# The first transposes of a graph-network stack taken from TensorE to blocked loads and VectorE

## The chip, the cores and the metric

The kernel runs on one core of one Trainium2 chip. The metric is device time in microseconds of one execution. The kernel before takes 1293.59 us, the median of three runs (1293.4 to 1294.62).

## The reference, cut to what matters

Four graph layers run over 64 independent graphs of 128 nodes with 256 features. Each is followed by a residual sum and a layer norm. Only the first touches what is changed here, apart from the adjacency, which all use:

```python
x:   (64, 128, 256) float32      adj: (64, 128, 128) float32, entries 0 or 1
qkv = x @ W_qkv                              # 8 heads of 64
attn = softmax(q @ k.T * scale) * 0.33 + 0.33 * adj + 0.33 * exp(-adj)     # masked
x = layernorm(x + (attn @ v) @ W_out + b_out)
# layer 1: H = (adj != 0), two hypergraph convolutions; layer 2: attention weights adj * exp(leaky(...)),
# two products with them; layer 3: adj @ (x @ W)
```

## The kernel before

The work goes in 32 groups of G = 2 graphs, and the engines follow orders written out by hand. One turn of the main loop (`group(i, j, n)` in each engine's block) holds the front half of group i (attention and first norm, F), the back half of group j = i - 1 (layers 1 to 3, B), and the lead of group n = i + 1 (L: x transposed and the first two of four query and key products). A function `first()` in each block takes the set-up, the weights, the front of group 0 and the lead of group 1. The turns with a lead after that are 30 (n from 2 to 31); then come one turn without a lead and one with a back half alone.

A product in float32 is made of three TensorE products of a float32r high part and low part of each operand: high times high, high times low, low times high (L405, L406, L409; for queries and keys L494, L495, L498). So whatever TensorE multiplies is copied once to a high part, by ScalarE, and once subtracted to a low part, mostly by VectorE.

TensorE contracts over partitions, so x and adj are needed transposed. Before, per group:

- `xT0_(n)` on TensorE (L483): four 128x128 transposes of `xin` into bank 0 of PSUM. ScalarE copies them to `xT0` high (L846), VectorE subtracts to `xT0` low (L1198, a helper's line, which the low parts of others share). `qk_(n, 0)`, `qk_(n, 1)` and, a turn later, `qk_(i, 2)`, `qk_(i, 3)` and `v_` read both.
- `adjT_(n)` on TensorE (L476): two transposes of `adj_in` into bank 6, after a wait for `dve_o3`. ScalarE copies them to `adjT` (L842), VectorE makes `HT` of it at the start of the next turn (`incidence`, L1222).

The orders in a turn around these, as far as the prediction's steps touch them:

- TensorE: ..., `xT2_(j)` (L604), `PT_(i, 0)` (L538), `xT0_(n)` (L483), `Z_(j, 0)`, `Z_(j, 1)` (L405, L406, L409), `si_(j, 0)`, `si_(j, 1)` (L632), `PV_(i, 0)` (L548), `qk_(n, 0)`, ..., `T3_(j, 0)`, `AT_(i)` (L513), `adjT_(n)` (L476), `T3_(j, 1)` (L661, L663, L665), ...
- VectorE: ..., `norm_(0, 1)` (four operations on L1285), `bn1_(0)` (L1347), `mv1_(0)` (L1208), `bn1_(1)`, `xT2_` (low part, L1198), `rl_`, `mv1_(1)`, `norm_(1, 0)`, `Z_(0)` (L1364, gives `sji`), `norm_(1, 1)`, `z0_(0)` (L1370), `Z_(1)` (L1364), `z2_(0)`, `xT0_` of n (low part), `z2_(1)`, ...; at the end `o3_(0)` (L1447), `zb_(1)` (L1203), ...
- GpSimd: `resid_` of the front (L1739), `resid_(0)`, `aT_`, `resid_(1)`, `gate_`, `rsh_`, then `rs1_(0)` and `rs1_(1)` (each L1722, L1726, L1732), `rs2_`, ...
- SyncE loads `xin` and the mask at the start of a turn, `adj_in` and `wrow` when their readers have finished, near its end (`reload`).

`si_(j, 1)` waits for `dve_sj` of `Z_(1)`; the low products in `Z_(j, 0)` wait for `dve_xT2`.

Of the kernel before, what the change touches and what calls it, by code (L numbers as in the profile page):

```python
# [5 lines left out]
F32 = mybir.dt.float32  # L6
# [3 lines left out]
ALU = mybir.AluOpType  # L10
# [16 lines left out]
def gnn_stack_kernel(nc, x, adj, nodemask, W_qkv, W_out, b_out, W1, b1, gamma, beta, W2, b2,  # L27
# [13 lines left out]
    QKB = 2 * INNER // P  # L41
    SCALE = float(DH) ** -0.5
# [3 lines left out]
    with ctx:  # L46
# [105 lines left out]
        adjT = at("adjT", [P, G, P])  # L152
        xT0 = pair("xT0", [P, DC, G, P])
# [33 lines left out]
        bank_adjT = 6  # L187
        bank_xT0 = 0
# [22 lines left out]
        def sem(name):  # L211
# [134 lines left out]

        block = ctx.enter_context(nc.Block())

        @block.sync
        def _(sp):  # L350
            sp.dma_start(wqkv_raw[:].rearrange("p c h t d -> p c (h t d)"),
                         W_qkv.rearrange("(c p) n -> p c n", p=P)).then_inc(ld_wqkv, 16)
            sp.dma_start(xin[:], xg[:, 0:G, :]).then_inc(x_in, 16)
            sp.dma_start(w2_raw[:], W2.rearrange("(c p) n -> p c n", p=P)).then_inc(ld_w2, 16)
            sp.dma_start(adj_in[:], ag[:, 0:G, :]).then_inc(a_in, 16)
            sp.dma_start(w1_raw[:], W1.rearrange("(c p) n -> p c n", p=P)).then_inc(ld_w1, 16)
# [11 lines left out]
            def reload(i):  # L368

                sp.wait_ge(pe_xT0, i)  # L370
                sp.wait_ge(pool_resid0, i)
                sp.sem_inc(sp_past, 1)
                sp.dma_start(xin[:], xg[:, bass.ds(i * G, G), :]).then_inc(x_in, 16)
                sp.wait_ge(act_mbc, i * G)
# [5 lines left out]
                sp.wait_ge(pe_adjT, i)  # L380
# [21 lines left out]
        def _(pe):  # L402
# [70 lines left out]
            def adjT_(i):  # L473
                pe.wait_ge(a_in, i * 16 + 16)
                for g in range(G):
                    last = pe.transpose(PS[:, bank_adjT, g * P:(g + 1) * P], adj_in[:, g, :], ident[:])  # L476
                last.then_inc(pe_adjT, 1)

            def xT0_(i):
                pe.wait_ge(x_in, i * 16 + 16)  # L480
                for c in range(DC):
                    for g in range(G):
                        last = pe.transpose(PS[:, bank_xT0, (c * G + g) * P:(c * G + g + 1) * P],  # L483
                                            xin[:, g, c * P:(c + 1) * P], ident[:])
                last.then_inc(pe_xT0, 1)

            def qk_(i, k):
                pe.wait_ge(act_xT0, i + 1)
                for m in range(2 * k, 2 * k + 2):
# [6 lines left out]
                    pe.wait_ge(dve_xT0, i + 1)  # L496
# [4 lines left out]
            def v_(i, g):  # L501
# [3 lines left out]
                pe.wait_ge(dve_xT0, i + 1)  # L505
# [161 lines left out]
            def group(i, j, n):  # L667
# [35 lines left out]
                if L:  # L703
                    after(pe, act_v, 2, s, 2)
                    xT0_(n)
# [13 lines left out]
                if L:  # L719
                    qk_(n, 1)  # L720
# [26 lines left out]
                if L:  # L747
                    after(pe, dve_o3, 2, s - 1, 1)
                    adjT_(n)
# [7 lines left out]
            def first():  # L757

                pe.wait_ge(ident_ok, 2)
                xT0_(0)  # L760
                w2_transposes()
                mask_column()
                pe.wait_ge(set_hi, QK_DONE)
# [54 lines left out]
        def _(act):  # L818
# [170 lines left out]
            def group(i, j, n):  # L989
# [74 lines left out]
                if L:  # L1064
                    adjT_(n)
# [796 lines left out]
```

## Time and profile before

| | |
|---|---|
| median of three runs | 1293.59 us (1293.4 to 1294.62) |
| span of the profiled execution | 1291.5 us |
| own time of the profiled execution | not listed apart from the three runs |
| TensorE busy | 1247.2 us, 97% |
| VectorE busy | 1068.8 us, 83% |
| ScalarE busy | 971.6 us, 75% |
| GpSimd busy | 478.5 us, 37% |
| mean granted TensorE clock | 0.993 |

A turn of the main loop takes 38.5 us; the one looked at is that from 640.0 to 678.5 us, in which the four engines are busy 38.27, 32.73, 29.97 and 14.66 us. The timeline gives for each instruction (or run of like ones, x4) its start, its length, engine, line, and what is written from what. Instructions of one engine overlap a little: what counts for the next is the distance from start to start. An idle stretch ahead of an instruction stands behind it in brackets, with what ended it.

### The profile page before, as it was taken

Reading aid. Unit: us, or ns where it says so; the run is one execution under the profiler, and the core shown is the slowest. Engines: PE = TensorE matmul, PEld = TensorE weight load, DVE = VectorE, ACT = ScalarE, POOL = GpSimd, SP = SyncE. Lnnn points to the kernel's source line nnn. Section 1 sums busy time; section 2 is a strip of 40 time slices with the busy share of each in tenths; the row PEclk is TensorE's granted clock in tenths of the full one; section 3 lists DMA queues with packets and bytes.
Section 4 is the critical chain, followed back from the end, with each engine's and each line's share of the span. In section 5 each row is a group of like instructions: output and inputs, shape, how many; then the busy total and the mean of one; then the engine's idle time right before and its main releaser. Section 6 shows DMA issues by size and latency. Waiting matters only on the chain.

```text
span 1291.5 us, 32910 instructions
## 1 busy us (share of the span) xinstructions
PE 1247.2 (97%) x9589; PEld 1110.3 (86%) x9589; DVE 1068.8 (83%) x3399; ACT 971.6 (75%) x2806; POOL 478.5 (37%) x1126
## 2 busy tenths in 40 slices
PE   6799999999999999999999999999999999999985
PEld 5688888888888888888898888898888898888874
DVE  3688888888888898888898888888888888888885
ACT  5477877777877777877777787778787777787773
POOL 3233444333443333443333343333343433344432
PEclk9899999999999999999999999999999999999998
DMA  6000100000000000000000100000001000000000
GB/s 214 17 8 21 26 25 25 16 16 18 25 25 25 22 11 17 25 25 25 25 9 17 25 25 25 25 8 19 23 25 25 25 8 23 20 25 25 17 9 9
DMA packets 44293, 32.52 MB, mean 25 GB/s; under 512 B 8176, under 2 KB 43120, under 8 KB 44272
## 3 DMA queue, kind: packets, MB, share of 16 engines
q1 hardware_dynamic: 42688, 31.47, 8.4%
q0 software_dynamic: 176, 0.52, 0.2%
q10 hardware_dynamic: 1408, 0.27, 0.1%
q8 instruction: 10, 0.16, 0.1%
q14 instruction: 11, 0.09, 0.0%
HBM read 23.87 MB, written 8.39 MB: 25 GB/s over the span
## 4 chain that ended last, share of the span: by engine, by line
PE 93%; DVE 3%; ACT 1%; issue 1%; DMA 1%; POOL 0%; DVEq 0%; SPq 0%; POOLq 0%; ACTq 0%
PE PS L405 15%; PE PS L406 15%; PE PS L409 15%; PE PS L494 5%; PE PS L548 5%; PE PS L495 5%; PE PS L498 5%; PE PS L528 4%; PE PS L538 4%; PE PS L584 3%; PE PS L568 2%; PE PS L598 2%; PE PS L520 2%; DVE ysb L1447 1%; PE PS L611 1%; PE PS L604 1%
## 5 line engine op out<-in xcount | busy, mean ns | idle before, releaser
L1722 POOL TENSOR_TENSOR rs<-mv,eps_c 128x1 f32<-128x1 f32 x256 | 61.2, 239 | 582.9 <-DVE mv L1208 581.4
L1726 POOL TENSOR_TENSOR rs<-rs,mhalf 128x1 f32<-128x1 f32 x320 | 176.3, 551 | 25.3
L891 ACT ACTIVATE prob<-PS,neg_max 128x128 f32<-128x128 f32 x512 | 179.7, 416 | 2.0 <-DVE neg_max L1272 2.0
L1285 DVE SCALAR_TENSOR_TENSOR prob<-prob,rl,gate 128x128 f32<-128x128 f32 x512 | 145.6, 347 | 1.5
L494 PE MATMUL PS<-xT_hi,wqk_hi 128*128 128x256 f32 x512 | 141.3, 297 | 0.0
L495 PE MATMUL PS<-xT_hi,wqk_lo 128*128 128x256 f32 x512 | 134.9, 285 | 0.0
L891 ACT ACTIVATION_READ_ACCUMULATOR prob<-PS,neg_max 128x1 f32 x512 | 131.4, 257 | 0.0
L1319 DVE SCALAR_TENSOR_TENSOR hid<-PS,Dn,b_bc 128x512 f32<-128x512 f32 x64 | 48.1, 751 | 85.4 <-PE PS L409 85.4
L498 PE MATMUL PS<-xT_lo,wqk_hi 128*128 128x256 f32 x512 | 103.5, 284 | 0.0
L494 PEld LDWEIGHTS PS<-xT_hi,wqk_hi 128*128 128x128 f32 x512 | 98.2, 192 | 5.3 <-issue 5.0
L495 PEld LDWEIGHTS PS<-xT_hi,wqk_lo 128*128 128x128 f32 x512 | 98.7, 193 | 0.0
L898 ACT ACTIVATE probT<-PS 128x1024 f32<-128x1024 f32 x64 | 65.9, 1029 | 32.0 <-PE PS L538 32.0
L909 ACT ACTIVATE x<-ysb,rs 128x256 f32<-128x256 f32 x128 | 73.5, 602 | 19.8 <-POOL rs L1732 19.8
L1732 POOL TENSOR_SCALAR rs<-mv,rs 128x1 f32<-128x1 f32 x256 | 68.2, 266 | 53.0 <-POOL rs L1726 52.6
L405 PE MATMUL PS<-wk_hi,xT_hi 128*128 128x260 f32 (+1 forms) x256 | 83.6, 348 | 0.7 <-ACT xT_hi L950 0.7
L406 PE MATMUL PS<-wk_lo,xT_hi 128*128 128x260 f32 (+1 forms) x256 | 83.4, 337 | 0.0
L498 PEld LDWEIGHTS PS<-xT_lo,wqk_hi 128*128 128x128 f32 x512 | 80.3, 192 | 0.0
L1272 DVE TENSOR_REDUCE neg_max<-PS 128x8 f32<-128x1024 f32 x64 | 77.9, 1219 | 1.9 <-PE PS L528 1.9
L1208 DVE BATCH_NORM_AGGREGATE mv<-st 128x2 f32<-128x6 f32 x320 | 56.5, 176 | 25.1 <-DVE st L1324 9.9
L874 ACT ACTIVATE qk<-PS 128x512 f32<-128x512 f32 x128 | 72.6, 591 | 5.3 <-PE PS L498 5.3
L909 ACT ACTIVATE xout<-ysb,rs 128x256 f32<-128x256 f32 x64 | 38.5, 601 | 47.2 <-POOL rs L1732 47.2
L1198 DVE TENSOR_TENSOR xT_lo<-PS,xT_hi 128x256 fp32r<-128x256 f32 (+1 forms) x128 | 70.5, 551 | 3.9 <-ACT xT_hi L846 1.8
(225 smaller groups left out, 4227.3 us busy)
## 6 DMA issues: line engine op xcount, KB each, us to landing
xin<-in_x_dram SPq DMA_DIRECT2D x32, 256.0 KB, 2.7
out_dram<-xout SPq DMA_DIRECT2D x32, 256.0 KB, 2.2
adj_in<-in_adj_dram SPq DMA_DIRECT2D x32, 128.0 KB, 2.1
wrow<-in_adj_dram SPq DMA_DIRECT2D x32, 128.0 KB, 4.5
wqkv_raw<-in_L_gnn_W_qkv_dram SPq DMA_DIRECT2D x1, 1536.0 KB, 7.6
w_raw<-in_L_gnn_W_dram SPq DMA_DIRECT2D x3, 512.0 KB, 11.4
mask_bc<-in_nodemask_dram SPq DMA_DIRECT2D x32, 32.0 KB, 2.8
wk_raw<-in_L_gnn_Wk_dram SPq DMA_DIRECT2D x3, 256.0 KB, 9.0
```

What stands on the lines that cost most here:

```text
L405: pe.matmul(dst, lhs[0], rhs[0], start=start, stop=False)
L406: pe.matmul(dst, lhs[0], rhs[1], start=False, stop=False)
L409: return pe.matmul(dst, lhs[1], rhs[0], start=False, stop=stop)
L494: pe.matmul(dst, w[0], xT0[0][:, c], start=(c == 0), stop=False)
L495: pe.matmul(dst, w[1], xT0[0][:, c], start=False, stop=False)
L498: last = pe.matmul(dst, wqk[0][:, c, t, h:h + 2], xT0[1][:, c], start=False, stop=(c == DC - 1))
L874: act.activation(qk[:, 2 * k:2 * k + 2].rearrange("p m g n -> p (m g n)"), PS[:, bank_qk[k], :], copy, scale=SCALE if k < 2 else 1.0).then ...
L891: last = act.activation(prob[:, t, h, :], PS[:, bank, k * P:(k + 1) * P], ACT.Exp, bias=neg_max[:, t, h:h + 1], accum_out=row_sum[:, t, h: ...
L909: act.activation(dst, src, ACT.Identity, scale=rs[:, n, g, 1:2], bias=rs[:, n, g, 0:1]).then_inc(done, 1)
L1272: dve.tensor_reduce(neg_max[:, t], scores, AX_X, ALU.max, negate=True).then_inc(dve_max, 1)
L1285: last = dve.scalar_tensor_tensor(prob[:, t, h, :], prob[:, t, h, :], rl[:, t, h:h + 1], gate[:, t], ALU.mult, ALU.add)
L1726: return pool.tensor_tensor(rs[:, n, g, 1:2], rs[:, n, g, 0:1], mhalf[:], ALU.pow)
```

## The change

x and adj are each loaded a second time, in blocks of 32x32: the block of rows 32a.. and columns 32k.. goes to partitions 32k.., to the place in the row that belongs to a. One VectorE `transpose`, which transposes inside each 32x32 block, then gives the whole transposed matrix in SBUF. The blocks come in runs of 32 floats (128 bytes), 2048 of them for x and 1024 for adj in a group, in four loads each. The low part of x goes from VectorE to GpSimd. The transposes on TensorE, their two PSUM uses, and ScalarE's copy of adj leave; ScalarE's copy to `xT0` high now reads SBUF.

```diff
+        Q = 32; QB = P // Q
+        def x_block(i, k):
+            return x[bass.ds(i * G, G)].rearrange("g (a r) (c k w) -> k r c (g a) w", r=Q, k=QB, w=Q)[k]
+        def adj_block(i, k):
+            return adj[bass.ds(i * G, G)].rearrange("g (a r) (k w) -> k r (g a) w", r=Q, k=QB)[k]
...
             # SyncE, set-up: after wqkv_raw, ahead of xin; and after adj_in
+            for k in range(QB):
+                sp.dma_start(xblk[k * Q:(k + 1) * Q], x_block(0, k)).then_inc(xb_in, 16)
...
             def reload(i):
-                sp.wait_ge(pe_xT0, i)
                 sp.wait_ge(pool_resid0, i)
                 sp.sem_inc(sp_past, 1)
                 sp.dma_start(xin[:], xg[:, bass.ds(i * G, G), :]).then_inc(x_in, 16)
+                sp.wait_ge(dve_xT, i)
+                for k in range(QB):
+                    sp.dma_start(xblk[k * Q:(k + 1) * Q], x_block(i, k)).then_inc(xb_in, 16)
+                sp.wait_ge(dve_adjT, i)
+                for k in range(QB):
+                    sp.dma_start(ablk[k * Q:(k + 1) * Q], adj_block(i, k)).then_inc(ab_in, 16)
                 sp.wait_ge(act_mbc, i * G)
...
             # TensorE
-                    pe.wait_ge(dve_xT0, i + 1)          # in qk_ and v_
+                    pe.wait_ge(pool_xT0, i + 1)
...
                 if F:
                     PT_(i, 0)
-                if L:
-                    after(pe, act_v, 2, s, 2)
-                    xT0_(n)
...
                 if L:
+                    after(pe, act_v, 2, s, 2)
                     qk_(n, 1)
...
                     AT_(i)
-                if L:
-                    after(pe, dve_o3, 2, s - 1, 1)
-                    adjT_(n)
...
             # ScalarE
             def xT0_(i):
-                act.wait_ge(pe_xT0, i + 1)
-                act.activation(xT0[0][:].rearrange("p c g n -> p (c g n)"), PS[:, bank_xT0, :], copy).then_inc(act_xT0, 1)
+                act.wait_ge(dve_xT, i + 1)
+                act.wait_ge(pe_v, i * G)
+                act.wait_ge(pool_xT0, i)
+                act.activation(xT0[0][:]..., xT[:]..., copy).then_inc(act_xT0, 1)
...
             # VectorE
+                def xT_():
+                    dve.wait_ge(xb_in, (i * QB + QB) * 16)
+                    dve.wait_ge(act_xT0, i)
+                    dve.wait_ge(pool_xT0, i)
+                    dve.transpose(xT[:]..., xblk[:]...).then_inc(dve_xT, 1)
                 def incidence():
-                    dve.wait_ge(act_adjT, i + 1)
+                    dve.wait_ge(ab_in, (i * QB + QB) * 16)
+                    dve.wait_ge(act_adjTb, i)
+                    dve.transpose(adjT[:]..., ablk[:]...).then_inc(dve_adjT, 1)
+                    dve.wait_ge(dve_adjT, i + 1)
+                    dve.wait_ge(act_BHT, i * G)
+                    dve.wait_ge(pe_AT, i)
                     dve.tensor_scalar(HT[:], adjT[:], 0.0, None, ALU.not_equal).then_inc(dve_HT, 1)
...
                     norm_(0, 1)
+                if L:
+                    front(n)[1]()                      # xT_
                 if B:
                     bn1_(0)
...
                     z2_(0)
-                if L:
-                    front(n)[1]()                      # the low part of x
                 if B:
                     z2_(1)
...
             # GpSimd
+                def xlow_():
+                    pool.wait_ge(act_xT0, i + 1)
+                    pool.wait_ge(pe_v, i * G)
+                    pool.tensor_tensor(xT0[1][:]..., xT[:]..., xT0[0][:]..., ALU.subtract).then_inc(pool_xT0, 1)
...
                     rs1_(1)
+                if L:
+                    front(n)[2]()                      # xlow_
+                if B:
                     rs2_(0)
```

In `first()` the same calls move: VectorE's `front(1)[1]()` keeps its place behind `centre_w3` and now is the transpose; ScalarE's `xT0_(1)` keeps its place ahead of `OT_(0, 0)`; GpSimd's low part for group 0 comes first and that for group 1 behind `gate_products`.

## Rows read from the trace of the kernel before

**Rows 1.** The page: TensorE's busy time, and the chain that ended last

```profile
PE 1247.2 (97%) x9589; PEld 1110.3 (86%) x9589; DVE 1068.8 (83%) x3399; ACT 971.6 (75%) x2806; POOL 478.5 (37%) x1126
...
PE 93%; DVE 3%; ACT 1%; issue 1%; DMA 1%; POOL 0%; DVEq 0%; SPq 0%; POOLq 0%; ACTq 0%
```

**Rows 2.** Timeline, TensorE, the middle of a turn: start us, length us, instruction

```profile
655.02 0.60 PE L483 MATMUL PS<-ident,xin 128*128 128x128 f32 x4
655.38 0.36 PE L405 MATMUL PS<-wk_hi,xT_hi 128*128 128x260 f32 x1
...
656.86 0.85 PE L409 MATMUL PS<-wk_hi,xT_lo 128*128 128x260 f32 x4
...
659.65 0.38 PE L632 MATMUL PS<-ident,sji 128*128 128x128 f32 x2
659.96 1.09 PE L548 MATMUL PS<-probT,vh 128*64 128x128 f32 x16
```

**Rows 3.** Timeline, ScalarE, the same stretch

```profile
654.41 0.65 ACT L950 ACTIVATE xT_hi<-PS 128x512 fp32r<-128x512 f32 x1
```

**Rows 4.** Timeline around `adjT_`, all engines

```profile
674.67 0.48 DVE L1203 SCALAR_TENSOR_TENSOR zb_lo<-PS,rs,zb_hi 128x256 fp32r<-128x256 f32 x1
674.79 0.20 PEld L476 LDWEIGHTS PS<-ident,adj_in 128*128 128x128 f32 x2 [0.42 <-DVE ysb L1447]
...
675.31 0.29 PE L665 MATMUL PS<-zb_lo,aT_hi 128*128 128x256 f32 x1
```

**Rows 5.** Timeline, VectorE, the middle of the turn

```profile
654.01 0.42 DVE L1347 BATCH_NORM_STATS2 st<-ysb 128x6 f32<-128x256 f32 x1
...
655.10 0.69 DVE L1198 TENSOR_TENSOR xT_lo<-PS,xT_hi 128x512 fp32r<-128x512 f32 x1
...
656.03 1.14 DVE L1285 SCALAR_TENSOR_TENSOR prob<-prob,rl,gate 128x128 f32<-128x128 f32 x4
...
657.44 1.13 DVE L1285 SCALAR_TENSOR_TENSOR prob<-prob,rl,gate 128x128 f32<-128x128 f32 x4
...
659.39 0.22 DVE L1364 SCALAR_TENSOR_TENSOR sji<-PS,rs,gate_c 128x4 f32<-128x4 f32 x1 [0.42 <-PE PS L409]
...
659.92 0.68 DVE L1198 TENSOR_TENSOR xT_lo<-PS,xT_hi 128x512 fp32r<-128x512 f32 x1
```

**Rows 6.** Groups of instructions by line and form, VectorE: busy us, mean ns, idle before

```profile
L1319 DVE SCALAR_TENSOR_TENSOR hid<-PS,Dn,b_bc 128x512 f32<-128x512 f32 x64 | 48.1, 751 | 85.4 <-PE PS L409 85.4
...
L1138 DVE TENSOR_REDUCE w3m<-w_raw 128x4 f32<-128x1024 f32 x1 | 1.2, 1214 | 0.0
...
L1131 DVE COPY beta_bc<-beta_c 128x512 f32<-128x512 f32 x1 | 0.4, 418 | 0.0
```

**Rows 7.** Timeline, GpSimd, the middle of the turn

```profile
654.85 0.19 POOL L1722 TENSOR_TENSOR rs<-mv,eps_c 128x1 f32<-128x1 f32 x1 [5.43 <-DVE mv L1208]
...
656.10 0.34 POOL L1722 TENSOR_TENSOR rs<-mv,eps_c 128x1 f32<-128x1 f32 x1
...
657.27 0.27 POOL L1732 TENSOR_SCALAR rs<-mv,rs 128x1 f32<-128x1 f32 x1 [0.21 <-POOL rs L1726]
```

**Rows 8.** Timeline, set-up: long GpSimd subtractions

```profile
44.84 3.77 POOL L1716 TENSOR_TENSOR wk_lo<-wk_raw,wk_hi 128x512 fp32r<-128x512 f32 x3 [14.96 <-DVE wk_raw L1155]
```

**Rows 9.** Timeline, VectorE, the same stretch

```profile
46.52 0.88 DVE L1173 TENSOR_TENSOR gate_c<-bsum,ab_bc 128x1 f32<-128x1 f32 x1
```

**Rows 10.** One line of the kernel: durations in ns, minimum, median, maximum

```profile
L1432 DVE TENSOR_SCALAR degb<-degf x32: 158/159/367, 60.3 to 1254.8; 128x2 f32<-128x2 f32 x32
```

**Rows 11.** DMA queues, and issues with us to landing

```profile
q1 hardware_dynamic: 42688, 31.47, 8.4%
...
xin<-in_x_dram SPq DMA_DIRECT2D x32, 256.0 KB, 2.7
...
mask_bc<-in_nodemask_dram SPq DMA_DIRECT2D x32, 32.0 KB, 2.8
```

**Rows 12.** The chain that ended last, set-up: start us, us, what

```profile
1.75 11.39 DMA w_raw<-in_L_gnn_W_dram
```

More of the change, by code:

```diff
@@ L41, in gnn_stack_kernel @@
     QKB = 2 * INNER // P
+    Q = 32
+    QB = P // Q
     SCALE = float(DH) ** -0.5
@@ L152, in gnn_stack_kernel @@
         adjT = at("adjT", [P, G, P])
+        ablk = at("ablk", [P, G * QB, Q])
+        xblk = at("xblk", [P, DC, G * QB, Q])
+        xT = at("xT", [P, DC, G * QB, Q])
         xT0 = pair("xT0", [P, DC, G, P])
@@ L373, in reload @@
                 sp.dma_start(xin[:], xg[:, bass.ds(i * G, G), :]).then_inc(x_in, 16)
+                sp.wait_ge(dve_xT, i)
+                sp.sem_inc(sp_past, 1)
+                for k in range(QB):
+                    sp.dma_start(xblk[k * Q:(k + 1) * Q], x_block(i, k)).then_inc(xb_in, 16)
+                sp.wait_ge(dve_adjT, i)
+                sp.sem_inc(sp_past, 1)
+                for k in range(QB):
+                    sp.dma_start(ablk[k * Q:(k + 1) * Q], adj_block(i, k)).then_inc(ab_in, 16)
                 sp.wait_ge(act_mbc, i * G)
@@ L471, in gate_sums @@
                 last.then_inc(set_pe, 1)
[L473 to L485, printed above, removed]
             def qk_(i, k):
@@ L759, in first @@
                 pe.wait_ge(ident_ok, 2)
-                xT0_(0)
                 w2_transposes()
@@ L765, in first @@
                 qk_(0, 0)
-                pe.wait_ge(dve_xT0, 1)
                 qk_(0, 1)
                 w1_transposes()
-                adjT_(0)
                 pe.wait_ge(set_copy, COPY_W2T)
@@ L785, in first @@
                 PT_(0, 0)
-                pe.wait_ge(act_v, 2)
-                xT0_(1)
                 PV_(0, 0)
@@ L790, in first @@
                 qk_(1, 0)
+                pe.wait_ge(act_v, 2)
                 qk_(1, 1)
@@ L801, in first @@
                 AT_(0)
-                adjT_(1)
                 pe.wait_ge(dve_y0, 2)
@@ L1079, in first @@
                 high(V_DONE, W1_DONE)
-                adjT_(0)
                 act.wait_ge(pool_const, 10)
@@ L1109, in first @@
                 ax_(0, 1)
-                adjT_(1)
             first()
@@ L1303, in mv0_ @@
                     aggregate(step, counted[t], NORM0, t, dve_mv0)
-                return (step, xT0_, incidence, cnt_, deg_, Be0_, Be_, Dsum_, Dn0_, Dn1_, Dn_, max_, rl_, norm_, OT_, y0_, bn0_,
+                return (step, xT_, incidence, cnt_, deg_, Be0_, Be_, Dsum_, Dn0_, Dn1_, Dn_, max_, rl_, norm_, OT_, y0_, bn0_,
                         mv0_)
@@ L1750, in rs0_ @@
                     scale_shift(step, NORM0, t, dve_mv0, i * G + t + 1, 2.0).then_inc(pool_rs0, 1)
-                return step, resid_, gate_, rs0_
+                def xlow_():
+                    pool.wait_ge(act_xT0, i + 1)
+                    pool.wait_ge(pe_v, i * G)
+                    pool.tensor_tensor(xT0[1][:].rearrange("p c g n -> p (c g n)"), xT[:].rearrange("p c b r -> p (c b r)"),
+                                       xT0[0][:].rearrange("p c g n -> p (c g n)").bitcast(F32), ALU.subtract)\
+                        .then_inc(pool_xT0, 1)
+                return step, resid_, xlow_, gate_, rs0_
             def back(j):
@@ L1780, in group @@
             def group(i, j, n):
-                F, B = i is not None, j is not None
+                F, B, L = i is not None, j is not None, n is not None
                 s = i if F else j + 1 if B else n - 1
                 if F:
-                    fstep, fresid_, gate_, rs0_ = front(i)
+                    fstep, fresid_, _, gate_, rs0_ = front(i)
                 if B:
@@ L1814, in first @@
             def first():
-                fstep, fresid_, gate_, rs0_ = front(0)
+                fstep, fresid_, xlow_, gate_, rs0_ = front(0)
                 pool.wait_ge(pool_const, 10)
+                xlow_()
                 pool.wait_ge(ld_vec, 16 * 3)
@@ L1821, in first @@
                 gate_products()
+                front(1)[2]()
                 low()
```

39 lines of the change are left out of this document (18 added, 21 removed).

## The prediction

> **What bounds the kernel now.** I read the page first, for the engine and for the chain that ended last: TensorE is busy 97% of the span and is 93% of that chain [rows 1]. So a turn of the main loop, 38.5 us, is worth what TensorE issues in it, and only what makes TensorE issue later or less counts. Then I read the timeline of TensorE where transposes leave, to see who stands behind them [rows 2 to 4], and that of VectorE and GpSimd where work comes in [rows 5, 7]. The reader is to see there how little lies between "VectorE is done" and "TensorE needs it": VectorE idles 0.42 us before the second `sji`, which TensorE's `si_` needs at once [rows 5, 2]. VectorE's large slack is elsewhere, before `hid`: 85.4 us in 64 waits, 1.33 us each [rows 6]. Last I looked for moments when GpSimd and VectorE work at the same time, since the change makes more of them [rows 8 to 10]. The profiled span is 1291.5 us and the median of the runs 2.1 us more. The sum is made on the span's turns and set on the median, the 2.1 us unchanged.
>
> **Transposes of x off TensorE.** The four of `xT0_` hold TensorE from 655.02 to 655.38, 0.36 us [rows 2]. `Z_(j, 0)` comes next and needs ScalarE's copy of `xT2`, which ends at 654.41 + 0.65 = 655.06 [rows 3]; with some 0.07 us to pass the semaphore it can start at 655.13. The gain is 0.25 us a turn, not 0.36.
>
> **Transposes of adj off TensorE.** They start at 674.79, after a wait for `ysb`, that is `o3_(0)`. But `T3_(j, 1)` behind them has a last product (675.31) that needs `zb_lo`, and VectorE makes it right behind `o3_(0)`, from 674.67 to 675.15 [rows 4]. Without the transposes this product starts at about 675.22. The gain is 0.09 us a turn, not the 0.4 that wait and transposes take. Their place is taken by the wait for `zb_lo`.
>
> **The transpose of x on VectorE.** No instruction of this kind is in the trace. A copy of 128x512 takes 0.42 us, a reduction of 128x1024, twice the columns, 1.21 us [rows 6]: these are the ends. The nearest is the subtraction of 128x512, one result a cycle, 0.69 us [rows 5]; I take that, and 0.60 us from start to start, as `xT_lo` gives way to the next instruction. The Trainium skill ("Vector Engine (DVE) Microarchitecture Reference", "The reshape front-end and per-opcode configuration") gives one element per cycle per lane for it, by which the sum would be the same.
>
> It takes over no slot: it stands ahead of `bn1_(0)` (654.01), the subtraction it replaces stood at 659.92 [rows 5]. So all VectorE work from 654.01 to 659.52 moves 0.60 us later. Who needs it? The low products of `Z_(j, 0)` start at 656.86, or 656.61 with the gain above; `xT_lo` of xT2 would end at 655.70 + 0.69 = 656.39 [rows 2, 5]: just in time. The second `sji` would start at 659.39 - 0.42 + 0.60 = 659.57 at the latest, or about 659.4, since the run of `norm_(1, 0)` (656.03 + 1.14 = 657.17) leaves 0.1 to 0.2 us before `norm_(1, 1)` at 657.44 [rows 5]. Before it started at 659.39 and `si_` at 659.65 [rows 2]. This would eat about 0.1 of the 0.25 us.
>
> **The low part of x on GpSimd.** Length: three subtractions of this form took 3.77 us, so 1.27 us each [rows 8]. Place: behind `rs1_(1)`, which ends at 657.27 + 0.27 = 657.54, and starts from `mv1_(0)`, which moves 0.60 us. So `xlow_` starts at about 658.1. TensorE needs its result only in `qk_(n, 0)`, behind `PV_` (659.96 and 1.0 us) [rows 2, 7]: over 1 us of slack, so as a dependency it costs nothing. But VectorE then is in `norm_(1, 1)`, four instructions that each read two SBUF tensors (`prob`, `gate`), moved from 657.44 to 657.9 and ending at about 659.0 [rows 5]. What happens then the trace shows three times. In set-up a VectorE instruction on 128x1 with two SBUF inputs took 0.88 us; it started at 46.52 in the middle of the second of GpSimd's subtractions and ended at 47.40, just as that did (44.84 + 2 x 1.27 = 47.38) [rows 8, 9]. `degb`, 0.16 us otherwise, once took 0.37 us beside a GpSimd add [rows 10]. And GpSimd's 0.19 us step takes 0.34 us where it falls on `norm_(1, 0)`, at 656.10 [rows 7]; it got in behind the first of the four, not behind all (656.03 to 657.17). So I take it that `xlow_` gets in behind one or two of the four and holds up the others for its whole length, 1.27 us. Bounds: nothing, if VectorE's run keeps it out; 1.3 us, its whole length.
>
> The page "SBUF — State Buffer" of the Trainium skill ("Who interferes with whom") states such a rule: a VectorE instruction with two SBUF inputs and a GpSimd instruction that reads SBUF exclude each other, and the one that issues first holds on for its whole length. By that rule, the trace agrees (0.88 us), and it speaks against this change.
>
> The price then: behind `norm_(1, 1)` come `z0_(0)` and the second `sji`, now at about 659.4 + 1.27 = 660.7, ending at 660.9. The second transpose of `si_`, which stood at 659.76 (0.11 behind the first) [rows 2], comes at 660.95 at best; TensorE's order is fixed, so `PV_` and all behind it wait. That is 1.15 us later than before, the 0.25 us included. With 0.09 us back from `adjT_` the turn grows by about 1.05 us; I take 1.0, since the 0.60 us step may be a little less. VectorE is 0.6 us relieved at 659.92 and is not late again.
>
> **The rest of a turn.** The transpose of adj (128x256, about 0.4 us) and the wait for its own end (some 0.16 us) stand before `hb_(0)`, covered by the 1.33 us of idle each [rows 6]; GpSimd's `ys` add of 1.3 us may hold up `dprod` there, covered too unless it starts late, then 0.1 us. ScalarE loses a copy and gains none. SyncE issues eight loads more a turn. Each load takes it about 0.4 us, so 3.4 us, behind `xin` at 642.6; behind them is the mask load, needed a turn later. 128-byte packets are not in the trace; an average packet (737 bytes) takes 8.4% x 16 x 1291.5 / 42688 = 41 ns, the upper bound, hence 2048 x 41 / 16 = 5.2 us for x, and landing takes 2.8 us for the small packets of the mask [rows 11]. Even so x is there by 642.9 + 1.7 + 5.2 + 2.8 = 652.6, before 654.0. Cost: nothing.
>
> **Set-up.** The chain there starts with the load of W2, landed at 13.14 us [rows 12]. Four loads with 256 KB go ahead of it: four issues of 0.46 us are 1.8 us, the bytes at the rate up to there (2304 KB in 12 us) 1.3 us; I take 1.7. ScalarE's copy of adj leaves its chain: -0.3. ScalarE's `xT0_(1)` must now wait for VectorE's transpose, and `OT_(0, 0)` behind it too, for which VectorE waits next: two copies of 0.65 us [rows 3], +1.3. Sum +2.7 us, bounds 0 and +6.
>
> **Sum.** 30 x 1.0 + 2.7 = 32.7 us on 1293.6: 1326.3 us. With the transpose at its ends (0.27 us less or 0.5 us more a turn) and the collision between 0.9 and 1.3 us, this case's own range is 1308 to 1342.
>
> **The rivals.**
>
> - **No collision: faster.** If VectorE's instructions, issued without a gap, keep GpSimd out until the four are done, `xlow_` runs from 659.0 to 660.3, beside instructions with one operand in PSUM (`z0_`, `sji`, `z2_`), and `qk_(n, 0)` still finds it ready. Then a turn gains 0.25 - 0.05 + 0.09 = 0.3 us: 1293.6 - 9 + 2.7 = 1287. It decides in `norm_(1, 1)`, and turns to a loss from a hold-up of about 0.3 us on. For it: the run of four beside the 0.34 us step is not longer than the next (1.14 and 1.13) [rows 5, 7]. Against it: that step read one column only, and it did get in.
> - **Half a collision: no change.** `xlow_` meets only the last instruction, or the hold-up is a part of its length; 0.2 to 0.4 us then cancels the gains, 1291 to 1297.
> - **A slow transpose without a collision.** At 1.21 us it makes `xT_lo` 0.3 us late for `Z_` and `sji` 0.5 us late: 30 x 0.25 + 2.7, so 1304.
> - **Late loads.** The Trainium skill ("VectorE: DVE Perf Modes", "The three transpose paths") warns that a plain DMA that transposes by strides is 19 times slower than the crossbar's where the innermost stride is large. Here the innermost run is contiguous. As a mechanism of this kernel, were the loads 19 times as slow as `xin`'s 2.7 us [rows 11], 51 us would stand where 11 (642.9 to 654.0) are free: 40 us a turn, some 2500 us. The mean packet of 41 ns speaks against it.
>
> **How the numbers follow.** Collision 0.70 (slower), none 0.20 (faster), half 0.05 (same), slow transpose 0.03, late loads 0.02 (both slower). Two cases of opposite sign hold most of the chance. I predict the likelier one, 1326 us. The range reaches down to the case without a collision, 1284, and up to 1340; outside are a bit of the upper end, late loads and the rival's lower end. 0.2%, or 2.6 us, is about what a measurement of this kernel tells from no change.
>
> **What would show it.** In the profile after: `norm_(1, 1)`'s run of four at 2.4 us instead of 1.13, `xlow_` beside it; TensorE idle 1.0 to 1.3 us before `si_` or `PV_`, released by `sji`; `z2_(0)` followed by `z2_(1)`; turns of 39.5 us. Were `norm_(1, 1)` still 1.1 us long, the rival is right. If VectorE idles before `transpose` for a load, the loads are the cause. Were `T3_`'s last product not waiting for `zb_lo`, my small gain for adj is wrong.

## The result, and the profile after

| | before | after |
|---|---|---|
| median of 4 runs each | 1293.49 us (1293.29 to 1294.62) | 1321.36 us (1320.99 to 1321.45) |
| profiled execution: time, span | 1293.6, 1291.5 us | 1321.37, 1319.6 us |
| a turn (start of the first `hid` to the next one's) | 38.49 | 39.24 |
| first `hid` (length of set-up) | 64.97 | 68.98 |
| last turn (nothing is prepared for a next one) | 35.54 | 37.10 |

After is slower: ratio 1.0213, 95% interval 1.0198 to 1.0227. The spans differ by 28.0 us before rounding, and the last three rows say where it is: 30 turns of 0.75 (22.3 by the stamps of the first and last `hid`), the last turn 1.55, set-up 4.0, and 0.1 behind the last `hid`. The turns repeat 30 times within a trace. Set-up and the last turn are read from one traced execution of each kernel, and the first `hid` came anywhere from 68.98 to 71.25 us in the six kernels that load in the order of the change (this one and experiments 1, 4, 5, 6 and 7, whose set-ups differ little), so set-up's 4.0 is known to some 2 us only.

The page of the kernel after: busy time, one queue, the chain that ended last (by engine, then by line), two groups of instructions and two loads.

```profile
PE 1242.3 (94%) x9397; PEld 1092.9 (83%) x9397; DVE 1116.4 (85%) x3431; ACT 959.8 (73%) x2774; POOL 534.5 (41%) x1158
...
q1 hardware_dynamic: 145088, 44.07, 14.5%
...
PE 83%; DVE 10%; ACT 3%; issue 2%; SPq 1%; DMA 0%; POOL 0%; DVEq 0%; POOLq 0%; ACTq 0%
PE PS L427 14%; PE PS L431 13%; PE PS L428 13%; DVE prob L1287 5%; PE PS L502 5%; PE PS L556 5%; PE PS L506 5%; PE PS L503 5%; PE PS L536 4%; PE PS L546 4%; PE PS L592 3%; PE PS L576 2%; PE PS L606 2%; PE PS L528 2%; ACT zb_hi L983 1%
...
L1287 DVE SCALAR_TENSOR_TENSOR prob<-prob,rl,gate 128x128 f32<-128x128 f32 x512 | 176.5, 406 | 1.5
...
L1321 DVE SCALAR_TENSOR_TENSOR hid<-PS,Dn,b_bc 128x512 f32<-128x512 f32 x64 | 48.0, 751 | 65.9 <-PE PS L431 65.9
...
xblk<-in_x_dram SPq DMA_DIRECT2D x128, 64.0 KB, 2.5
...
ablk<-in_adj_dram SPq DMA_DIRECT2D x128, 32.0 KB, 1.9
```

Against [rows 1], TensorE is busy 5 us less and carries 83% of the chain instead of 93%; VectorE has risen from 3% to 10%, and half of that is one group: `norm_`'s `prob`, which the page of before doesn't list there. The same 512 instructions were 145.6 us on the page of before (347 ns each) and are 176.5 us now (406 ns). 31 us were put on them, and no edit touches them. The DMA queue carries 3.4 times as many packets [rows 11], and yet the loads land in 2.5 and 1.9 us.

The middle of a turn, VectorE's timeline of the kernel after (start us, length us, instruction), answers to [rows 5]:

```profile
669.21 0.70 DVE L1212 STREAM_TRANSPOSE xT<-xblk 128x512 f32<-128x512 f32 x1
669.84 0.38 DVE L1349 BATCH_NORM_STATS2 st<-ysb 128x6 f32<-128x256 f32 x1
...
671.71 1.15 DVE L1287 SCALAR_TENSOR_TENSOR prob<-prob,rl,gate 128x128 f32<-128x128 f32 x4
672.77 0.22 DVE L1366 SCALAR_TENSOR_TENSOR sji<-PS,rs,gate_c 128x4 f32<-128x4 f32 x1
672.91 2.17 DVE L1287 SCALAR_TENSOR_TENSOR prob<-prob,rl,gate 128x128 f32<-128x128 f32 x4
675.00 0.47 DVE L1372 SCALAR_TENSOR_TENSOR z<-PS,rs,bk_bc 128x256 f32<-128x256 f32 x1
675.39 0.20 DVE L1366 SCALAR_TENSOR_TENSOR sji<-PS,rs,gate_c 128x4 f32<-128x4 f32 x1
```

GpSimd's timeline of the same stretch, which answers to [rows 7]:

```profile
672.95 0.61 POOL L1734 TENSOR_SCALAR rs<-mv,rs 128x1 f32<-128x1 f32 x1 [0.20 <-POOL rs L1728]
673.53 1.40 POOL L1758 TENSOR_TENSOR xT_lo<-xT,xT_hi 128x512 fp32r<-128x512 f32 x1
```

And TensorE's, which answers to [rows 2]:

```profile
670.32 0.39 PE L427 MATMUL PS<-wk_hi,xT_hi 128*128 128x260 f32 x1
...
674.62 0.27 PE L640 MATMUL PS<-ident,sji 128*128 128x128 f32 x1
675.66 0.32 PE L640 MATMUL PS<-ident,sji 128*128 128x128 f32 x1 [0.77 <-DVE sji L1366]
675.91 1.09 PE L556 MATMUL PS<-probT,vh 128*64 128x128 f32 x16
```

`norm_(1, 1)`, the second run of four, is 2.17 us long; it was 1.13. In narrower windows its first three instructions start at 672.91, 673.17 and 673.43 and last 0.34 us each, and the fourth, started at 673.70, lasts 1.38: 1.04 us too many. It ends at 675.08, some 0.14 behind `xlow_` (673.53 + 1.40 = 674.93). The second `sji`, which idled 0.42 us for TensorE before, is now itself what TensorE waits for. TensorE's waits, one row of the kernel after for each of the two that are new; columns are us in total, times, longest:

```profile
PE PS L640 <- DVE sji L1366: 23.2, 30, 0.9
...
PE PS L673 <- DVE zb_lo L1196: 12.3, 32, 0.4
```

30 waits of 0.77 us for `sji` are new, one in each turn with a lead. The turn's growth of 0.75 is a net figure: this wait and the 0.38 us for `zb_lo` came in, the transposes and their wait went out. What the collision alone costs is in experiment 1.

### The profile page after: what moved, and what is told of

It is laid out like the page before. It is cut to its first block, busy times and chain, and to the rows that moved or that the text cites. A ratio compares the mean times of both kernels' runs of the same rounds, so it can differ in the third digit from the quotient of the medians.

```text
span 1319.6 us, 33509 instructions
## 1 busy us (share of the span) xinstructions
PE 1242.3 (94%) x9397; PEld 1092.9 (83%) x9397; DVE 1116.4 (85%) x3431; ACT 959.8 (73%) x2774; POOL 534.5 (41%) x1158
## 4 chain that ended last, share of the span: by engine, by line
PE 83%; DVE 10%; ACT 3%; issue 2%; SPq 1%; DMA 0%; POOL 0%; DVEq 0%; POOLq 0%; ACTq 0%
PE PS L427 14%; PE PS L431 13%; PE PS L428 13%; DVE prob L1287 5%; PE PS L502 5%; PE PS L556 5%; PE PS L506 5%; PE PS L503 5%; PE PS L536 4%; PE PS L546 4%; PE PS L592 3%; PE PS L576 2%; PE PS L606 2%; PE PS L528 2%; ACT zb_hi L983 1%
## 5 line engine op out<-in xcount | busy, mean ns | idle before, releaser
L1728 POOL TENSOR_TENSOR rs<-rs,mhalf 128x1 f32<-128x1 f32 x320 | 176.5, 551 | 25.3
L1287 DVE SCALAR_TENSOR_TENSOR prob<-prob,rl,gate 128x128 f32<-128x128 f32 x512 | 176.5, 406 | 1.5
L1734 POOL TENSOR_SCALAR rs<-mv,rs 128x1 f32<-128x1 f32 x256 | 81.2, 317 | 53.0 <-POOL rs L1728 52.6
L556 PE MATMUL PS<-probT,vh 128*64 128x128 f32 x1024 | 70.6, 280 | 2.3 <-ACT probT L895 2.3
```

The lines of the kernel that those rows point to most:

```text
L556: last = pe.matmul(PS[par * DH:(par + 1) * DH, bank_PV[t], k * P:(k + 1) * P], vh[:, t, 2 * k + par, :], probT[:, t, par * (HEADS // 2) + ...
L1287: last = dve.scalar_tensor_tensor(prob[:, t, h, :], prob[:, t, h, :], rl[:, t, h:h + 1], gate[:, t], ALU.mult, ALU.add)
L1728: return pool.tensor_tensor(rs[:, n, g, 1:2], rs[:, n, g, 0:1], mhalf[:], ALU.pow)
L1734: return pool.tensor_scalar(rs[:, n, g, 0:1], mv[:, n, g, 0:1], rs[:, n, g, 1:2], -1.0, ALU.mult, ALU.mult)
```

## The experiments

My theory: the hold-up of `norm_(1, 1)` by `xlow_` through their reads is all of the turn's loss, and without it the change would win about 0.25 us a turn. Rivals: the added work on VectorE (the 0.60 us step) is the loss; any work on GpSimd at that place would do it; the loss comes with adj or the loads.

**1. `xlow_` behind the run of four.** One wait more in `xlow_`:

```diff
                     pool.wait_ge(pe_v, i * G)
+                    pool.wait_ge(dve_attn, i * 2 * G)
```

> The kernel after, with one wait more: GpSimd's subtraction of x starts only when VectorE has finished the four instructions of norm_(1, 1). Theory (collision at the port between the two engines): norm_(1, 1) takes 1.13 us again instead of 2.17, the second sji comes 1.04 us earlier, the second transpose of si_ 0.93 us earlier (675.66 less 674.73, where TensorE would be ready). A turn of 38.3 us instead of 39.24, 30 x 0.93 = 28 us less: 1293.5 us (1291 to 1296). Rival (VectorE is slowed by the loads' traffic or by its own transpose): the run of four stays at 2.2 us, and the time at 1321 us or a little more.

1292.82 us (1291.41 to 1293.29, 11 runs), ratio to before 0.9993 (0.9984 to 1.0002). One wait gives back 28.5 us. VectorE's timeline of this kernel:

```profile
658.66 1.15 DVE L1287 SCALAR_TENSOR_TENSOR prob<-prob,rl,gate 128x128 f32<-128x128 f32 x4
659.73 0.21 DVE L1366 SCALAR_TENSOR_TENSOR sji<-PS,rs,gate_c 128x4 f32<-128x4 f32 x1
659.86 1.13 DVE L1287 SCALAR_TENSOR_TENSOR prob<-prob,rl,gate 128x128 f32<-128x128 f32 x4
660.91 0.48 DVE L1372 SCALAR_TENSOR_TENSOR z<-PS,rs,bk_bc 128x256 f32<-128x256 f32 x1
```

GpSimd's:

```profile
661.07 1.29 POOL L1759 TENSOR_TENSOR xT_lo<-xT,xT_hi 128x512 fp32r<-128x512 f32 x1 [0.56 <-DVE prob L1287]
```

TensorE's:

```profile
661.56 0.38 PE L640 MATMUL PS<-ident,sji 128*128 128x128 f32 x2
```

The run is 1.13 us again and the two transposes of `si_` go together, without a wait, though the stream transpose and its 0.60 us are still there. The same subtraction (1.29 us) now lies beside `z`, `sji` and `z_lo`, which have one operand in PSUM, and holds up none of them (0.48, 0.22 and 0.48 us, the same as before). The turn is 38.25 us: 0.99 less than in the kernel after, 0.24 less than before. The loss of the turns is the place of `xlow_`; the loads and VectorE's transposes, all still there, make none of it. The kernel is no faster than before because in this trace set-up (first `hid` at 70.76) and the last turn (36.99) took 7.2 us of what 30 turns gave.

**2. Before, with a read on GpSimd.** The kernel before, with this behind `rs1_(1)`:

```diff
                     rs1_(1)
+                if L:
+                    pool.tensor_tensor(probe[:], b1_bc[:], b1_bc[:], ALU.subtract).then_inc(pool_probe, 1)
```

> The kernel before, unchanged but for one GpSimd subtraction of 128x512 with both inputs in SBUF, behind rs1_(1), into a tile that nothing reads. It starts at about 657.5 in the turn that was shown, where norm_(1, 1) starts at 657.44. Theory: the run of four takes 2.2 us instead of 1.13, of the 1.04 us 0.42 is VectorE's idle time before the second sji, so TensorE waits 0.6 us a turn: 30 x 0.6 = 18 us, 1311.5 us (1307 to 1316). Rival (the slow run needs the blocked loads or the transpose): 1293.5 us.

1304.02 us (1300.79 to 1304.27, 4 runs), ratio 1.0081 (1.0066 to 1.0096). Slower, so a read on GpSimd alone makes such a loss in a kernel that has nothing else of the change; but less of it than I expected, and outside my 1307 to 1316. VectorE's timeline:

```profile
660.20 1.92 DVE L1287 SCALAR_TENSOR_TENSOR prob<-prob,rl,gate 128x128 f32<-128x128 f32 x4
662.04 0.47 DVE L1372 SCALAR_TENSOR_TENSOR z<-PS,rs,bk_bc 128x256 f32<-128x256 f32 x1
662.43 0.21 DVE L1366 SCALAR_TENSOR_TENSOR sji<-PS,rs,gate_c 128x4 f32<-128x4 f32 x1
```

GpSimd's:

```profile
660.26 1.19 POOL L1804 TENSOR_TENSOR probe<-b_bc 128x512 f32<-128x512 f32 x1
```

The probe got in behind the first of the four; the second, started at 660.46, lasted 1.13 us, 0.79 too many, and ended 0.14 us behind the probe, as in the kernel after. The turn is 38.68, 0.19 more, where I expected 0.6. I had already taken off VectorE's 0.42 us of idle time. Of the missing 0.4, 0.25 is the shorter hold-up (0.79 and not 1.04). Another 0.09 is that from start to start the idle stretch gave 0.51: the second `sji` started 4.29 us behind the first product of `Z_`, against 4.01 before, so 0.28 of the 0.79 reached it. The last 0.09 went between `sji` and the next `hid`. The turns (5.8 us) and a last turn of 37.10 make the profiled 1300.8; three further runs took 1303.8 to 1304.3, and what their 3 us are no trace shows.

**3. Before, with writes alone on GpSimd.** At the same place:

```diff
+                    for _ in range(3):
+                        pool.memset(probe[:, _ * DHID:(_ + 1) * DHID], 0.0).then_inc(pool_probe, 1)
```

> The kernel before, with three GpSimd memsets of 128x512 at the same place instead of the subtraction: about as long, but they read nothing from SBUF. If only a GpSimd instruction that reads SBUF keeps VectorE's second input out, the run of four stays at 1.13 us and the time at 1293.5 us (1292 to 1295.5). Rival (any GpSimd instruction that long does it): as with the subtraction, 1307 to 1316 us.

1294.22 us (1291.99 to 1294.64, 10 runs), ratio 0.9999 (0.9989 to 1.0008). GpSimd's timeline, then VectorE's:

```profile
656.20 1.46 POOL L1805 MEMSET probe<- 128x512 f32 x3
```

```profile
656.20 1.13 DVE L1287 SCALAR_TENSOR_TENSOR prob<-prob,rl,gate 128x128 f32<-128x128 f32 x4
```

1.46 us of GpSimd exactly beside the run of four, and it is 1.13 us. So it isn't GpSimd's being busy. What the probe of experiment 2 has and these don't is reads of SBUF (and one long instruction instead of three of 0.49 us; but experiment 7 shows that shorter ones that read still hold VectorE up).

**4. adj back on TensorE.** `adjT_` stands again on TensorE and ScalarE, and the blocked loads and VectorE's transpose of adj are gone; x stays as in the change.

```diff
-                for k in range(QB):
-                    sp.dma_start(ablk[k * Q:(k + 1) * Q], adj_block(i, k)).then_inc(ab_in, 16)
...
+                if L:
+                    after(pe, dve_o3, 2, s - 1, 1)
+                    adjT_(n)
```

> The kernel after, with the adjacency's part undone: its two transposes are on TensorE again, its blocked loads and VectorE's transpose of it are gone. Theory: TensorE only waits for zb_lo 0.38 us less where the transposes stand again, so the part is worth 0.09 us a turn, and without it the time is 30 x 0.09 = 2.7 us more, less up to 1.5 us of set-up that the eight loads cost: 1322.5 us (1320 to 1325). Rival (the transposes and their wait cost what they show, 0.4 us a turn): 1333 us.

1320.69 us (1320.08 to 1321.78, 5 runs), ratio 1.0208 (1.0194 to 1.0222). The time is in the range but the reason isn't: the turn is 39.23 us against 39.24, so the adj half is worth nothing, not 0.09. TensorE of the kernel after:

```profile
651.93 0.39 PE L673 MATMUL PS<-zb_lo,aT_hi 128*128 128x256 f32 x1 [0.38 <-DVE zb_lo L1196]
652.15 1.07 PE L576 MATMUL PS<-hbh,x1t 128*128 128x128 f32 x7
```

ScalarE:

```profile
651.97 0.60 ACT L906 ACTIVATE x1t<-ys,rs 128x256 f32<-128x256 f32 x1 [0.27 <-POOL rs L1734]
```

The wait for `zb_lo` did take the place of the transposes, as predicted. But `ax_` behind it reads `x1t` in its last products, and that comes from ScalarE, released by GpSimd's `rs`: a chain that doesn't pass through TensorE's transposes. The fifth product of `ax_` starts 0.05 us behind the end of `x1t` in both kernels (675.91 behind 675.86 before, 652.62 behind 652.57 after), and from the start of `x1t` to the `qk_` behind `ax_` it is 1.13 us before, 1.12 after and 1.13 with adj back. I stopped at the first wait behind the removed instructions; the second one decides.

**5. The low part of x on VectorE**, behind `z2_(0)`, where it stood before; the stream transposes stay.

```diff
                     z2_(0)
+                if L:
+                    front(n)[18]()                      # xlow_, now a VectorE instruction
```

> The kernel after, with the low part of x back on VectorE, at its old place between z2_(0) and z2_(1), now with both inputs in SBUF; GpSimd has no work more than in the kernel before. Theory: nothing collides with norm_(1, 1), so it takes 1.13 us; VectorE's 0.6 us for the low part stood at this place before without anyone waiting. A turn of 38.25 us as with the wait added, 1293.5 us (1291 to 1296). Rival (VectorE, with both the transposes and the low part, is now the bound): 0.3 to 0.6 us more a turn, 1302 to 1311 us.

1293.94 us (1293.45 to 1294.44, 10 runs), ratio 1.0003 (0.9994 to 1.0013); turn 38.28. That is experiment 1 within 0.03 us a turn: even without the collision, moving the subtraction to GpSimd wins no more than that.

**6. The subtraction twice**, in `xlow_` of the kernel after, one behind the other:

```diff
                     pool.tensor_tensor(xT0[1]..., xT..., xT0[0]..., ALU.subtract).then_inc(pool_low1, 1)
+                    pool.wait_ge(pool_low1, i + 1)
+                    pool.tensor_tensor(xT0[1]..., xT..., xT0[0]..., ALU.subtract).then_inc(pool_xT0, 1)
```

> The kernel after, with GpSimd's subtraction of x done twice, one behind the end of the other; TensorE waits for the second. The second would run from about 1.5 to 2.9 us behind the start of the first, beside z0_, sji and z2_ on VectorE, each of which takes an input from PSUM. Theory (only VectorE instructions with two SBUF inputs are held): the run of four stays at 2.17 us, the second subtraction holds nobody, and 1321.4 us stays (1320 to 1324). Rival (any GpSimd instruction that reads holds VectorE up): z0_ or sji are held again, 1 us more a turn, 1345 to 1352 us.

1321.85 us (1320.59 to 1323.55, 4 runs), ratio 1.0212 (1.0195 to 1.023); turn 39.23. VectorE's run, then GpSimd:

```profile
675.15 2.17 DVE L1288 SCALAR_TENSOR_TENSOR prob<-prob,rl,gate 128x128 f32<-128x128 f32 x4
```

```profile
675.77 1.40 POOL L1759 TENSOR_TENSOR xT_lo<-xT,xT_hi 128x512 fp32r<-128x512 f32 x1
677.25 1.27 POOL L1763 TENSOR_TENSOR xT_lo<-xT,xT_hi 128x512 fp32r<-128x512 f32 x1
```

Twice the work costs nothing more: the second lies beside instructions with an operand in PSUM, and `qk_` has the slack for it (it starts 1.03 us behind `PV_`, 1.02 in the kernel after). It isn't how much GpSimd reads, but beside what.

**7. The subtraction in halves**, 128x256 each:

```diff
-                    pool.tensor_tensor(xT0[1]..., xT..., xT0[0]..., ALU.subtract).then_inc(pool_xT0, 1)
+                    for c in range(DC):
+                        last = pool.tensor_tensor(xT0[1][:, c]..., xT[:, c]..., xT0[0][:, c]..., ALU.subtract)
+                    last.then_inc(pool_xT0, 1)
```

> The kernel after, with GpSimd's subtraction of x cut into two of 128x256 (0.73 us each). In the kernel after the fourth instruction of norm_(1, 1) was held 1.04 us. Theory (the port is held for one instruction): the fourth instruction gets in behind the first half and is held about half as long, 0.4 to 0.6 us; the run takes 1.6 us, a turn 38.7 us instead of 39.24, the time 1305 us (1301 to 1310). Rival (GpSimd keeps the port over instructions that follow each other without a gap): no change or, with two fixed parts, a little more, 1321 to 1326 us.

1304.44 us (1303.31 to 1305.33, 4 runs), ratio 1.0078 (1.0061 to 1.0095), as expected. VectorE, GpSimd, and TensorE's wait for it:

```profile
665.30 1.61 DVE L1287 SCALAR_TENSOR_TENSOR prob<-prob,rl,gate 128x128 f32<-128x128 f32 x4
```

```profile
665.92 1.58 POOL L1759 TENSOR_TENSOR xT_lo<-xT,xT_hi 128x256 fp32r<-128x256 f32 x2
```

```profile
PE PS L640 <- DVE sji L1366: 7.2, 30, 0.3
```

The fourth instruction is held 0.48 us instead of 1.04, by one half. The turn is 38.67. So the length of the single instruction that is under way sets the price. VectorE gets in between two GpSimd instructions, even where they follow each other without a gap.

**8. Set-up.** To experiment 1 I added the order of loads (W2 ahead of the blocked x, `xin` behind W1) and moved VectorE's transpose for group 1 from behind `centre_w3` to behind `centre`.

```diff
+            sp.dma_start(w2_raw[:], W2.rearrange("(c p) n -> p c n", p=P)).then_inc(ld_w2, 16)
             for k in range(QB):
                 sp.dma_start(xblk[k * Q:(k + 1) * Q], x_block(0, k)).then_inc(xb_in, 16)
...
                 centre()
+                front(1)[1]()
```

> The kernel after with GpSimd's wait for norm_(1, 1), and with set-up reordered: W2's load goes ahead of the blocked loads of x, the plain x behind W1; VectorE transposes x of group 1 before the attention's norms of group 0, so that ScalarE doesn't wait for it. Theory: turns of 38.25 us as before, W2 lands at 13.1 us instead of 15.0, ScalarE's wait of 1.3 us goes: 3 us less than with the wait alone, 1289.8 us (1287 to 1292). Rival (set-up's length comes from the bytes, or from TensorE's clock, not from these two): 1292.8 us, no change.

1289.83 us (1287.96 to 1291.02, 6 runs), ratio 0.9968 (0.9955 to 0.998). The total came as expected; its parts didn't. W2 landed at 11.83 us, earlier than the 13.1 I wrote, but the last block of x at 14.75 instead of 13.43, and the first query and key product, which needs x, moved only from 17.87 to 16.29. The first `hid` is 1.1 us earlier than in experiment 1 (69.66); in experiments 9 and 10, with the same order of the first loads, it came at 67.02 and 67.18. TensorE's granted clock from 30 to 45 us was 0.81 in this trace and 1.00 in those two. And 1.44 us of the gain is the last turn (35.55), which nothing in this edit touches.

**9. The same with adj back on TensorE** (experiments 4 and 8 together).

> As the last, with the adjacency's part undone (its transposes on TensorE, no blocked loads of it). Theory: that part moves the time by nothing, since TensorE waits at this point for x1t, whichever stands ahead: turns of 38.25 us, 1289.8 us, or up to 1.5 us less through shorter set-up (1286 to 1292). Rival (it is worth 0.09 us a turn): 2.7 us more than the last.

1290.07 us (1288.46 to 1290.54, 7 runs), ratio 0.9969 (0.9958 to 0.9981). I expected the same as in 8, and no 2.7 us more. Turn 38.25, last turn 35.55, as in 8: adj's half of the change can be left out at no loss.

**10. The transpose early.** Experiment 8, with `xT_` between `Dsum_(0)` and `hb_(0)`, where VectorE waits for TensorE anyway, and with the blocked loads for it a turn ahead.

```diff
                 if F:
                     Dsum_(0)
+                if L:
+                    front(n)[1]()
                 if B:
                     hb_(0)
```

> As e9_late_low_setup, with VectorE's transpose of x at the start of the turn, in its idle time before hb_(0) (1.33 us each before), and the blocked loads of x issued at the end of the turn before for it. It undoes the 0.60 us by which all VectorE work in the middle of the turn came later. Theory: nobody waits for that work once the collision is gone, so the turn stays at 38.25 us and the time is that of the last but one, 1289.8 us (1287 to 1292). Rival (the 0.60 us are on the path): 0.1 to 0.3 us less a turn, 1281 to 1287 us.

1289.44 us (1288.28 to 1291.75, 8 runs), ratio 0.9971 (0.996 to 0.9981). VectorE's timeline of this kernel:

```profile
655.79 1.12 DVE L1294 SCALAR_TENSOR_TENSOR prob<-prob,rl,gate 128x128 f32<-128x128 f32 x4
...
657.67 0.22 DVE L1373 SCALAR_TENSOR_TENSOR sji<-PS,rs,gate_c 128x4 f32<-128x4 f32 x1 [0.36 <-PE PS L438]
```

`sji` idles for TensorE again, 0.36 us against the 0.42 of [rows 5], and the turn is 38.25 as in 8, as I expected. So the 0.60 us step costs nothing where `xlow_` doesn't collide; it only uses up the idle time that would have softened the collision.

## Why the prediction was right, and where its terms were off

The sign and the cause came as forecast: slower, by a hold-up of `norm_(1, 1)` that TensorE waits for. That 1321.4 lies between 1284 and 1340 says less, since that range holds the case without a collision too. And that the sum came within 5 us of the time is partly luck: the turns were forecast 7.7 us too dear, and 3 us of set-up and last turn that no step had made up for part of it.

**x off TensorE: right.** 0.25 us a turn predicted; 0.24 measured in experiments 1, 8 and 10 (38.49 against 38.25), as the whole gain of a turn without the collision. That rests on `Z_` waiting for the copy of `xT2` and not on the 0.36 us that the transposes held. In the kernel after, ScalarE's copy ends at 669.61 + 0.65 = 670.26, and `Z_` starts at 670.32:

```profile
669.61 0.65 ACT L947 ACTIVATE xT_hi<-PS 128x512 fp32r<-128x512 f32 x1
```


**adj off TensorE: wrong by its whole size.** 0.09 predicted, 0.00 (experiments 4 and 9). The wait for `zb_lo` came as I wrote; the wait for `x1t` behind it I didn't look at. Over 30 turns that is 2.7 us.

**The transpose of x: right.** 0.69 us and 0.60 from start to start taken; 0.70 and 0.63 (669.21 to 669.84) measured. One element per cycle and lane, as the Trainium skill gives ("Vector Engine (DVE) Microarchitecture Reference", "The reshape front-end and per-opcode configuration"), agrees with 0.70 us for 512 columns, the length of the subtraction in [rows 5], and 0.44 us for the 256 of adj. The step down the queue was less than 0.60 by the second run of `norm_`, though: from the start of `Z_` to that run was 2.06 us [rows 2, 5] and is 672.91 - 670.32 = 2.59, which with the 0.25 gained is 0.28 later than before, where I had 0.46.

**The collision: right in place, kind and culprit, 0.23 us too large.** I took 1.27, the whole of `xlow_`; the hold-up was 1.04, and it held the fourth instruction, where I had it get in behind one or two. `xlow_` starts while the third of the four is in work, and what lies beside that one costs nothing; only from where the fourth would begin does VectorE wait. It got in behind the third, not behind the first or second, since GpSimd's own `rs` step before it took 0.61 us instead of 0.27 (the GpSimd rows above, and [rows 7]). In experiment 2 that step ended as the run began (0.27 us), and the probe got in behind the first. The rule in the Trainium skill ("SBUF — State Buffer", "Who interferes with whom"), that a VectorE instruction with two SBUF inputs contends with a GpSimd instruction that reads SBUF and not with one that only writes it, is borne out: 1.04 us in the kernel after, 0.79 in experiment 2, none in 3, none beside instructions with a PSUM operand in 1 and 6. The prediction gave it as holding for the whole length; that section of the Trainium skill says "for the whole instruction" of VectorE's two-port modes and doesn't say it of two SBUF inputs. Here the hold-up was 1.04 of 1.40 and 0.79 of 1.19 us. The instruction held did end just behind GpSimd's each time; what makes the hold-up shorter is the part of GpSimd's that lay beside the VectorE instruction already in work, and the held one's own 0.34 us.

One of the prediction's three signs doesn't fit the rule on two inputs: `degb` [rows 10] reads a single SBUF tensor (`degf`, 128x2), and yet it took 0.37 us and ended at 60.71, 0.02 behind a GpSimd add (59.95 + 0.74 = 60.69). It happened once in 32 times; no run here looks at why.

**The turn.** Predicted for the second transpose of `si_`: 660.95 against 659.76, which is 1.19 us later (the prediction's 1.15 is a slip, and its 1.05 a turn was rounded down to 1.0). Measured from the start of `Z_`: 4.38 before (659.76 - 655.38), 5.34 after (675.66 - 670.32), less the 0.25 gained, 0.71 later. Of the missing 0.48, 0.23 is the hold-up, 0.18 the earlier run, and the rest 0.07 is in the steps between. With nothing back from adj the turn grew 0.75 and not 1.0, so 30 turns 22.3 us and not 30.

**Set-up: too small.** +2.7 predicted, +4.0 measured, inside my bounds of 0 and 6. The first term was right in size: W2 landed at 15.0 instead of 13.1, 1.9 us where I had 1.7. The chain that ended last, kernel after, set-up:

```profile
1.25 0.74 SPq L366
...
4.42 2.63 SPq L366
7.09 2.64 SPq L367
9.78 5.25 DMA w_raw<-in_L_gnn_W_dram
```

The chain runs through SyncE's issuing: the four blocked loads hold it for 5.8 us and `xin` for another 2.6, against 0.46 us for `xin` before. Whether the issuing itself or the bytes queued ahead of it take the time isn't shown; in the kernel before, too, an issue was held 2.91 us (the mask's, at 3.86, behind the first loads). The second term is there as well: the chain passes through VectorE's transpose and ScalarE's copy behind it, 0.63 us each, where I had 1.3 for two copies. What is left over is about 1 us. The granted clock is no sure cause of it. From 30 to 45 us it was 1.00 before and 0.89 after, which is 1.7 us of full clock; but in experiments 5 and 7 it was 1.00 in that stretch, and the first `hid` came no earlier (69.98 and 69.79). From 45 to 75 us both kernels lost the same in sum (0.84 and 0.93 before, 0.99 and 0.78 after).

**The last turn: missing.** 1.55 us that no step of mine had. The windows tell it; columns are stretch, us, then busy us and count by engine, granted clock, DMA share, GB/s. Before:

```profile
1240.00:1244.30 4.30, 3.47 (x28) 3.23 (x28) 4.16 (x16) 2.22 (x5) 0.00 (x0) 1.00 0.00 0
```

After, in the same place of the last turn:

```profile
1268.00:1272.30 4.30, 4.30 (x26) 4.30 (x25) 2.67 (x11) 2.04 (x5) 0.00 (x0) 0.60 0.01 2
```

The granted clock was 0.60 of full in these 4.3 us, so part of them was run at 1.2 GHz, and products of 128x256 follow each other by 0.21 us instead of 0.12. The share lost, 0.4 of 4.3 us, is 1.7 us, about the whole of the 1.55. TensorE had idled 0.92, 0.42 and 0.40 us just before, in both kernels alike. The last turn is as long (36.99 to 37.11) in experiments 1, 2, 4, 5, 6 and 7, and 35.5 in 3, 8, 9 and 10; over 15 us around the drop the clock was 0.90 in experiment 1 and 1.00 in 8. Experiment 2 is the kernel before with a probe, so it isn't the transposes that bring it. What tips it is open: with one traced execution of each kernel it may be the execution and not the kernel, and over whole executions the mean granted clock of the kernel before itself differed from 0.990 to 0.993.

**The other side.** The rival without a collision had 1287 us; with the collision alone taken away, the turns gain what it says (0.24 against 0.3), and the total stands at 1292.8 because set-up and last turn cost 7.2 instead of 2.7. What spoke against it, that a GpSimd step had got in behind the first of four, was the evidence that decided. The slow transpose and the late loads didn't happen: 0.70 us, and 2.5 us from issue to landing. The sum of 32.7, against 28.0 between the spans, is short by the last turn (+1.55), by set-up (+1.3) and by 0.1 at the end, and over by the turns (-7.7).

**Faster than both.** Experiments 8 to 10, at 1289.4 to 1290.1 us, are 0.3% faster than before, their intervals below 1, and 2.4% faster than after. Of the 3 us that they are ahead of experiment 1, 1.4 is the short last turn, whose cause is open. The simplest is experiment 9: x alone off TensorE, `xlow_` behind the run of four, and set-up in the order of experiment 8.

## What to carry to other kernels

Before giving GpSimd a tensor operation, list VectorE's instructions that lie beside it and ask of each whether both its inputs are in SBUF (`degb` shows that this question may not find all of them); if VectorE has one that TensorE needs soon, let the GpSimd operation start behind it with one wait, or cut it into pieces. When work is taken off the bound engine, follow its queue to the second wait behind the removed instructions and not only to the first. Count what a load costs its issuing queue apart from when it lands, above all at the start of the kernel, where other loads stand behind it.

## What the runs showed of the hardware that I had not expected

- The hold-up is shorter than the GpSimd instruction: 1.04 us of 1.40, 0.79 of 1.19, 0.48 for a half. Each time the held VectorE instruction ended 0.14 or 0.15 us behind GpSimd's.
- It goes both ways in one run: the GpSimd step on one column took 0.61 us instead of 0.27 beside the first instructions of VectorE's run, and then GpSimd's long one got in. Four VectorE instructions issued without a gap didn't keep it out in any of these runs.
- An issue holds SyncE longer the more pieces the load has: in the turns of the kernel after 0.58 us for one of x's blocked loads (64 KB in 512 pieces), 0.32 for one of adj's (32 KB in 256 pieces) and 0.38 for `xin` (256 KB in long rows). SyncE's queue in a turn, where the four of x take 0.74 us each with what lies between them; I had 0.4:

```profile
657.96 0.38 SPq L388 DMA_DIRECT2D xin<-in_x_dram  x1
658.52 2.95 SPq L392 DMA_DIRECT2D xblk<-in_x_dram  x4
```

  In set-up, behind the 1.5 MB of the first load, the fourth held SyncE 2.63 us.
- TensorE's granted clock in a stretch differed between the traces of two kernels with the same gaps on TensorE just before it: 1.00 and 0.60 in the last turn.
